# Cross-attention with routed experts: the first head group's maxima move into the projections, later groups' maximum rows travel by one copy and four transfers

## The reference, cut to what matters

```python
y_dca, y_main = y[:, -16:, :], y[:, :-16, :]      # y is the context: 16 and 496 rows
q = ln(x_norm @ Wq + bq, per head)                # 512 queries
k, v = ln(y_main @ Wk + bk), y_main @ Wv + bv     # 496 keys
k_dca, v_dca = ln(...), ...                       # 16 keys, of weights of their own
ctx = softmax(q k^T * 32**-0.5) v + softmax(q k_dca^T * 32**-0.5) v_dca
x = x + ctx @ Wo + bo
x = x + ffn(layernorm(x))                         # 7 routed experts, top 2, and one shared
```

## Time and profile before

| | |
|---|---|
| median of 3 runs | 995.12 us (993.21 to 996.1) |
| profiled execution | 995.3 us; its span in the trace 993.6 us |
| TensorE busy | 909.5 us, 92% of the span |
| VectorE, ScalarE, GpSimd busy | 636.0, 459.5, 563.9 us |
| mean granted clock of TensorE | 0.962 of full |

### The profile page before, as it was taken

The page is one execution under the profiler, slowest core; times in us unless marked ns, Lnnn a source line. Parts: engine busy times, 40 slices in busy tenths (PEclk is TensorE's granted clock), DMA queues, the critical chain, the costliest instruction groups (busy, mean ns, idle before and its releaser), DMA issues. The chain is left out here.

```text
span 993.6 us, 16827 instructions
## 1 busy us (share of the span) xinstructions
PE 909.5 (92%) x5047; PEld 406.6 (41%) x5048; DVE 636.0 (64%) x1019; ACT 459.5 (46%) x846; POOL 563.9 (57%) x487
## 2 busy tenths in 40 slices
PE   3889895799999999989999689999999999999898
PEld 1345442122221222246644245555555555555443
DVE  7888777588787988467776144554554444443388
ACT  3375665678877888722353022332233233323540
POOL 5465556367777775543127499989999920000372
PEclk9798998599999999999999799999999999999999
DMA  7234635445454532133425766666566643335676
GB/s 233 77 92 122 179 105 166 139 158 169 167 177 159 177 105 70 53 107 128 153 112 218 289 191 209 217 200 220 201 215 205 201 139 106 121 109 187 232 203 221
DMA packets 106059, 162.26 MB, mean 163 GB/s; under 512 B 12536, under 2 KB 55608, under 8 KB 105616
## 3 DMA queue, kind: packets, MB, share of 16 engines
q1 hardware_dynamic: 92768, 115.86, 35.9%
q0 software_dynamic: 12896, 45.10, 13.6%
q10 hardware_dynamic: 336, 0.57, 0.2%
HBM read 107.88 MB, written 53.48 MB: 162 GB/s over the span
## 5 line engine op out<-in xcount | busy, mean ns | idle before, releaser
L1089 ACT ACTIVATE p_t<-a_psT 128x512 f32<-128x512 f32 x256 | 138.9, 595 | 47.4 <-PE a_psT L1212 46.1
L1136 DVE TENSOR_REDUCE nm<-quad 128x4 bf16<-128x1984 f32 x60 | 133.9, 2231 | 35.7 <-PE quad L1197 35.7
L1905 ACT ACTIVATE e_xT<-quad 128x512 f16<-128x512 f32 x38 | 22.7, 597 | 229.9 <-PE quad L1969 229.9
L1979 PE MATMUL quad<-w_exp,e_xT 128*128 x456 | 107.2, 386 | 4.9 <-DVE e_xT L1933 2.6
L1039 POOL TENSOR_TENSOR p_sum<-p_t,p_t 128x512 f32<-128x512 f32 x64 | 81.1, 1275 | 53.2 <-ACT p_t L1089 53.0
L1979 PE MATMUL quad<-w_exp,e_uT 128*128 x456 | 104.6, 379 | 0.0
L1979 PE MATMUL e_psY<-w_exp,e_gT 128*128 x456 | 104.6, 379 | 0.0
L1212 PE MATMUL a_psT<-q_stk,k_stk 98*128 98x512 f16 x256 | 84.6, 401 | 11.2 <-ACT p_t L1089 9.4
L215 POOL TENSOR_TENSOR w_exp<-e_raw,w_exp 128x1024 f16<-128x1024 f32 x42 | 91.7, 2184 | 3.5
L1936 DVE SCALAR_TENSOR_TENSOR e_g<-quad,bias 128x512 f32<-128x512 f32 x38 | 26.3, 691 | 85.4 <-PE e_psGT L1969 80.5
L1936 DVE SCALAR_TENSOR_TENSOR e_u<-quad,bias 128x512 f32<-128x512 f32 x38 | 26.3, 691 | 73.9 <-PE quad L1979 73.9
(11 more groups left out here) (338 smaller groups left out, 1797.0 us busy)
## 6 DMA issues: line engine op xcount, KB each, us to landing
xs_dram<-zero SPq DMA_DIRECT2D x38, 256.0 KB, 6.9
bias<-in_L_ffn_bup_dram SPq DMA_DIRECT2D x38, 256.0 KB, 3.3
bias<-in_L_ffn_bgate_dram SPq DMA_DIRECT2D x38, 256.0 KB, 3.4
ys_dram<-e_y SPq DMA_DIRECT2D x38, 256.0 KB, 2.0
e_x<-xs_dram SPq DMA_DIRECT2D x36, 256.0 KB, 2.8
q_dram<-q_st SPq DMA_DIRECT2D x24, 256.0 KB, 3.0
k_dram<-k_st SPq DMA_DIRECT2D x24, 256.0 KB, 3.6
q_stk<-q_dram SPq DMA_DIRECT2D x64, 96.0 KB
```

Source lines behind the costliest of these rows:

```text
L1089: act.activation(probs(w, k), psT[:, k % 2], ACT.Exp, scale=SCALE / (QS * QS)).then_inc(s["exp"], 1)
L1136: dve.tensor_reduce(nm[:, i, :, 0:1].rearrange("p h o -> p (h o)"), psS[:, :, 0:NMAIN], AX.X, ALU.max, negate=True)
L1979: ins = pe.matmul(dst[:, :], stationary, moving, start=(k == 0), stop=(k == len(terms) - 1))
```

## The change

Group 0's scores are computed one head and one block at a time in `psD` by `first_score`, 16 in all, two for each of the last eight blocks of the projections; `first_max` reduces each. `first_max_rows` and four copies of ScalarE make group 0's rows inside `project`. The early scores now are those of group 1, blocks 0 and 1. `first_heads` is issued in batch 1 instead of the last one. In `attend`, ScalarE copies all of `psX` to a tile `m_row` once for each later group, and SP carries each head's two rows to `q_stk` by a transfer of its own, behind the loads of the group's fourth head. TensorE's order of turned pairs and sums is shifted by one place. Two loops that ran in hardware (VectorE, SP) are written out.

```diff
-MAX_EARLY = 4
+MAX_EARLY = 2
@@ project: first_heads
             for q in st_q + st_k:
-                sp.wait_ge(q, 3 * 16 * (B - 1))
+                sp.wait_ge(q, 3 * 16)
...
-                    if last and j == 1:
+                    if b == 1 and j == 2:
                         first_heads(sp)
@@ project: ScalarE, at the end
             back(B - 1, TB - 2)
+            act.wait_ge(g_["m_mm"], 1)
+            for h in range(HEAD_GROUP):
+                act.activation(g_["q_stk"][3 * HD:3 * HD + 2, h, :], psK[h * HD:h * HD + 2, :], ACT.Copy, scale=1.0 / QS).then_inc(g_["mrow"], 1)
             back(B - 1, TB - 1)
@@ project: VectorE, in mid behind the eviction of v, and in steps between front_a and front_c
+                if b >= B - 2:
+                    first_max(first_of(b, j) + 1)
...
+            def first_max(n):
+                i, h = divmod(n, HEAD_GROUP)
+                dve.wait_ge(g_["first_mm"], n + 1)
+                nm = g_["nm"][:, i, h, 0:2]
+                dve.tensor_reduce(nm[:, 0:1], psD[:, 0:NMAIN], AX.X, ALU.max, negate=True)
+                dve.tensor_reduce(nm[:, 1:2], psD[:, NMAIN:S], AX.X, ALU.max, negate=True).then_inc(g_["first_max"], 1)
...
+                    if b >= B - 2:
+                        first_max(first_of(b, j))
@@ project: TensorE, in mid behind the products of q, and in back between the turns of q and k
+                if b >= B - 2:
+                    first_score(first_of(b, j))
...
+                    if src is kn and between is not None:
+                        first_score(between)
...
+            def first_score(n):
+                i, h = divmod(n, HEAD_GROUP)
+                at_least(pe, g_["first_max"], n)
+                at = slice(h * HD, (h + 1) * HD)
+                pe.matmul(psD[:, :], g_["q_hi"][at, 0, i * P:(i + 1) * P], g_["k_hi"][at, 0, :], start=True, stop=True,
+                          tile_position=(h * HD, 0)).then_inc(g_["first_mm"], 1)
@@ attend: SP
+                if u % G == G - 1 and u >= G:
+                    sp.wait_ge(s["mrow"], copied(u // G))
+                    for h in range(G):
+                        sp.dma_start(q_stk[K3:KR, h, :], m_row[h * HD:h * HD + 2, :]).then_inc(row_put, 16)
@@ attend: ScalarE, once a group instead of four times max_row
+            def max_copy(gr):
+                act.wait_ge(s["m_mm"], gr + 1)
+                at_least(act, row_put, rows_of(gr - 1))
+                act.activation(m_row[:, :], psX[:, :], ACT.Copy, scale=1.0 / QS).then_inc(s["mrow"], 1)
@@ attend: TensorE
             def scores_t(w, k):
                 if k == 0:
                     pe.wait_ge(loaded[w % SLOTS], 32 * (w // SLOTS + 1))
-                    pe.wait_ge(s["mrow"], w + 1)
+                    at_least(pe, row_put, rows_of(w // G))
@@ attend: TensorE, the order of a period
                     scores(new, 1)
+                turned_pair(now, 0, 0)
                 if scored(old):
                     sums(old)
-                turned_pair(now, 0, 0)
+                turned_pair(now, 0, 1)
                 if scored(old):
                     third_sums(old)
                 if scored(new) and new:
                     scores(new, 2)
-                turned_pair(now, 0, 1)
+                turned_pair(now, 1, 0)
                 if scored(old):
                     last_sums(old)
-                turned_pair(now, 1, 0)
+                turned_pair(now, 1, 1)
                 if scored(old):
                     values(old, 2)
                 if scored(new) and new:
                     scores(new, 3)
-                turned_pair(now, 1, 1)
+                turned_pair(now, 2, 0)
                 if scored(old):
                     dca(old)
-                turned_pair(now, 2, 0)
+                turned_pair(now, 2, 1)
                 if scored(old):
                     values(old, 3)
-                turned_pair(now, 2, 1)
                 turned_pair(now, 3, 0)
```

More of the change, by code:

```diff
@@ L184, in build @@
         seen_max = sem("a_max")
+        first_mm = sem("a_first_mm")
+        first_max = sem("a_first_max")
+        m_mm = sem("a_m_mm")
+        mrow = sem("a_mrow")
         xs_zeroed = sem("xs_zeroed")
@@ L356, in w_view, with first_of @@
             return w.rearrange("p (h two d) -> p h two d" if natural else "p (two h d) -> p h two d", two=2, d=HD)
+        def first_of(b, j):
+            return 2 * (g_of(b, j) - (B - 2) * TB)
         def k_cols(w):
@@ L417, in _ @@
                              vf[b * NDCA:(b + 1) * NDCA, :].rearrange("p (h d) -> p h d", d=HD)).then_inc(s["dca_v_st"], 16)
-            with sp.Fori(1, B - 1) as b:
+            for b in range(1, B - 1):
                 steps(b, False)
@@ L817, in _ @@
             dca_norm()
-            with dve.Fori(1, B - 1) as b:
+            for b in range(1, B - 1):
                 steps(b, False, False)
             steps(B - 1, False, True)
-            dve.wait_ge(s["masks"], 6)
             for i in range(MAX_EARLY):
@@ L894, in dca_keys_turn, with back @@
                 ins.then_inc(s["dca_kT_t"], 1)
-            def back(b, j):
+            def back(b, j, between=None):
                 g = g_of(b, j)
                 for src, dst, rdy, used, dn in ((qn, psQT, "qn_r", "qa_r", "qT_t"), (kn, psKT, "kn_r", "ka_r", "kT_t")):
+                    if src is kn and between is not None:
+                        first_score(between)
                     pe.wait_ge(s[rdy], g + 1)
@@ L906, in back, with first_max_rows @@
                     ins.then_inc(s[dn], 1)
+            def first_score(n):
+                i, h = divmod(n, HEAD_GROUP)
+                if n == 0:
+                    pe.wait_ge(g_["hi_loaded"][0], 32)
+                    pe.wait_ge(s["dca_kT_r"], 1)
+                at_least(pe, g_["first_max"], n)
+                at = slice(h * HD, (h + 1) * HD)
+                pe.matmul(psD[:, :], g_["q_hi"][at, 0, i * P:(i + 1) * P], g_["k_hi"][at, 0, :], start=True, stop=True,
+                          tile_position=(h * HD, 0)).then_inc(g_["first_mm"], 1)
+            def first_max_rows():
+                pe.wait_ge(g_["first_max"], TB * HEAD_GROUP)
+                pe.wait_ge(s["k_ev"], NT)
+                for q in range(TB):
+                    ins = pe.matmul(psK[:, q * P:(q + 1) * P], g_["nm"][:, q, :, :].rearrange("p h o -> p (h o)"), ident_b[:, :], start=True, stop=True)
+                ins.then_inc(g_["m_mm"], 1)
             def early_scores(i):
                 if i == 0:
-                    pe.wait_ge(g_["hi_loaded"][0], 32)
+                    pe.wait_ge(g_["hi_loaded"][1], 32)
+                    pe.wait_ge(g_["first_max"], TB * HEAD_GROUP)
                     pe.wait_ge(s["q_ev"], NT)
@@ L916, in early_scores @@
                     at = slice(h * HD, (h + 1) * HD)
-                    ins = pe.matmul(psS[:, h], g_["q_hi"][at, 0, i * P:(i + 1) * P], g_["k_hi"][at, 0, :], start=True, stop=True, tile_position=(h * HD, 0))
+                    ins = pe.matmul(psS[:, h], g_["q_hi"][at, 1, i * P:(i + 1) * P], g_["k_hi"][at, 1, :], start=True, stop=True, tile_position=(h * HD, 0))
                 ins.then_inc(g_["s_mm"], 1)
@@ L932, in steps @@
                         dca_keys_turn()
+                    between = first_of(b, j) + 1 if b >= B - 2 else None
                     if last and j == TB - 1:
+                        back(b, j - 1, between)
                         early_scores(0)
-                    if j:
-                        back(b, j - 1)
+                        first_max_rows()
+                    elif j:
+                        back(b, j - 1, between)
                     elif not first:
-                        back(b - 1, TB - 1)
+                        back(b - 1, TB - 1, between)
             front(0, 0)
@@ L988, in scored, with rounds, copied, rows_of @@
             return 0 <= p < NG
+        def rounds(p):
+            return TB * (p - 1)
+        def copied(gr):
+            return G + gr
+        def rows_of(gr):
+            return 16 * G * gr
         def probs(n, k):
@@ L1106, in _ @@
                 n = early_of(p)
-                if scored(p - 1):
-                    for h in range(G):
-                        max_row(G * (p - 1) + h)
+                if scored(p - 1) and p - 1:
+                    max_copy(p - 1)
                 pair(p - 2, TB - 1, 1)
@@ L1132, in maxima @@
             def maxima(p, i):
-                dve.wait_ge(s["s_mm"], TB * p + i + 1)
-                at_least(dve, s["m_mm"], p)
+                if p == 1 and i < MAX_EARLY:
+                    return
+                dve.wait_ge(s["s_mm"], rounds(p) + i + 1)
+                dve.wait_ge(s["m_mm"], p)
                 dve.tensor_reduce(nm[:, i, :, 0:1].rearrange("p h o -> p (h o)"), psS[:, :, 0:NMAIN], AX.X, ALU.max, negate=True)
@@ L1190, in scores @@
             def scores(p, i):
+                if p == 1 and i < MAX_EARLY:
+                    return
                 if i == 0:
```

(7 more changed lines are left out.)

20 lines of the change are left out of this document (10 added, 10 removed).

## The result

The changed kernel takes 1085.8 us (median of 4 runs, 1084.13 to 1086.3) against 994.2 us before: ratio 1.091, 95% interval 1.0891 to 1.0929. The profiled execution took 1086.3 us with a span of 1084.6 us.

A forecast was written before the change was run, and what follows sets the result against it. TensorE was taken as the busiest engine, its waits deciding; a period grows from 15.09 to 19.1 us, fifteen cost 60 more. Sum: 995.3 - 6.6 + 60 = 1048.7, say 1049 us; range 1014 to 1086.

The forecast's parts named there:

- The rival with the deep queue: Attention: in ten periods with stores of zeros, transfers land 9.5 us after the group's last turned pair; 1088 us, chance 0.09.
- The landing: Between groups: the fourth transfer lands at T + 6.0 (4.9 to 9.5), T being the end of a group's last turned pair.
- The body of a turn: TensorE in attention: the rest of a period's work, from the next group's first turned pair to its last, takes 11.8 us.
- The clock: TensorE behind the new wait: drops to half clock in most periods, 1.3 us each (0 to 1.7).
- The row's full value: Profile of the kernel before: TensorE work at 1.2 GHz behind two waits, worth 1.7 us at full clock.
- VectorE's rival: Attention: transfers are cheap, VectorE sets a period of 15.1 us, 6 us won at the head; 989 us, chance 0.06.
- The forecast point of decision: Between groups: cheap transfers decide from a landing 3.7 us after the last turned pair, where fifteen periods cost 6.6 us.
- The end of `project`: End of the projections: the barrier moves from 174.88 to about 174.1, a gain of 0.8 us.
- The cover of the maxima: VectorE in `project`: waits hide most of the sixteen `first_max`, leaving 2.2 us; without any cover 12 us.
- I count nothing: Batch 1: earlier `first_heads` holds SP some 9 us, taken as no cost, 3 us if cover is thin.
- the first group: Start of attention: takes 11.5 us instead of 17.36, a gain of 5.8 us.
- the four row copies: ScalarE ahead of the last block's turned k and q: four copies delay GpSimd's last subtraction by 1.4 us.

The follow-up runs named there:

- (5): Changed kernel with two row transfers in place of four, same 8 KB, still behind the fourth head's loads: 1078.4 us.
- (8): Changed kernel with the row transfers issued by ScalarE on its own queue, SP issuing loads only: 1083.6 us.
- (4): Changed kernel with the four row transfers issued ahead of the fourth head's two loads instead of behind them: 1036.2 us.
- experiment 6: Changed kernel with two row transfers in place of four, issued ahead of the fourth head's loads: 1020.7 us.
- the warm kernel: Changed kernel with twelve products of overwritten result filling most of TensorE's wait for the transfers: 1060.6 us.
- (1): Changed kernel with four ScalarE row copies again and no transfers; new TensorE order and head part stay: 997.5 us, ratio 1.0017.
- head-only: Changed kernel with four ScalarE row copies and TensorE's old order, so only the head part is left: 996.1 us, ratio 1.0006.
- (10): Head part alone in three steps: alone 996.1 us; eight stack loads back in the last batch 988.6 us; then row copies last 989.6 us.
- the split one: Head part alone, with the eight stack loads of `first_heads` back in the last batch: 988.6 us, ratio 0.9932 of the kernel before.

## Why the prediction was right, and where it was off

Slower was forecast, for the reason that holds: four transfers that start at T, land about T + 6 and hold TensorE's queue, with the clock at half behind them. The size, 1049, was 37 us short of 1086, at the very edge of the range, and that it still lay inside is luck: three terms of a turn were each too small, and all in the same direction. The rival with the deep queue had 1088, nearer in number but not in kind: it wanted T + 9.5 in ten turns, and only the first turn came to that. By the prediction's own steps:

- *The landing.* Forecast T + 6.0; measured 6.0 to 6.3 in the last five turns, a mean of 6.8 over nine with zeros, 9.4 in the first, 6.8 over all fifteen. The reason given, that the first transfer queues behind head 3's loads and the fourth lands with it, held: half the issues changed the landing by 0.2 us or so (5), another queue not at all on the mean of the turns with zeros (6.8 in both, 8), a place ahead of the loads by 2.4 where no zeros are (4). The issue was 0.62 us each, not 0.48, which mattered little for that reason. As the prediction also had it, the queue is on the DMA engines and not SP's (8). The zeros were put among the rivals only; they cost 0.7 us in each of nine turns. Term: +0.8 us a turn.
- *The body of a turn.* Forecast 11.8 us from the pair to T. At full clock it is 12.4 (389.22 to 401.66 in the kernel of experiment 6). The 0.56 us wait for ScalarE did go, as said, but the step missed that another comes with the spread order: 0.75 us for `scaled_dca` ahead of `max_rows`, in 14 turns. +0.6.
- *The clock.* Forecast 1.3 us in most turns. What is left of the turn is 21.1 - 6.8 - 12.4 = 1.9; the warm kernel gives 1.7. The row's full value was the better one. Every wait here was 3.3 us or more and the clock fell behind each, though not always at once (the pair at 414.71 took 0.59 us, and the granted clock over the 3.5 us from there was 0.68). +0.6. These three make the 2.0 us a turn between 19.1 and 21.1, 30 us.
- *VectorE's rival.* The pair at T + 3.3 and a turn of 15.1 us if the transfers cost nothing; measured T + 2.7 and 15.22 (1), 15.13 to 15.26 (6). The forecast point of decision, a landing at T + 3.7, was reached in turns without zeros (3.67 in 4, 2.7 in 6) and in some with them (3.3 in 6).
- *The end of `project`.* Forecast 174.1, measured 180.7. The cover of the maxima held: a block takes 7.9 us where it took 7.85. The step that failed is "I count nothing" for the earlier `first_heads`, with 3 us if cover is thin: it cost 5.3 us of waiting for x and 1.4 (head-only) to 2.8 us (changed) of low clock behind that wait. With the stack loads away (10) the rest of the step came out: attention starts at 173.6 (forecast 174.1), the first group takes 11.9 us (forecast 11.5), and it ends at 185.5, where 192.24 - 6.6 = 185.6 was the forecast. Only the four row copies, taken at 1.4, cost 0.34. The first exponential, expected 3 to 5 us earlier, is 2.4 us later in the changed kernel (182.09, before 179.72) and 4.7 us earlier in the split one (175.02).

30 us from the turns and 7.4 from the head are the 37.6 us between 1048.7 and the profiled 1086.3.

What the change wins is at the head, some 6 to 7 us, and it was hidden by the load order there; later groups' transfers gain nothing over four copies by any form tried. Even where the transfers vanish a turn in the new order is about 15.1 us: TensorE's 14.0 us of work and two waits for VectorE, 0.35 us for the maxima and 0.75 us for `scaled_dca`. VectorE itself stands for 2.1 us of such a turn (386.40 to 401.66 in experiment 6), each time for TensorE's scores, so it is the chain between the two that sets the pace. The new order gives nothing here, and the 1.9 us that ScalarE saves have no taker. The old order with one copy and hidden transfers was not tried.

Open: how the zeros hold the transfers, and why longer in some turns than in others (experiment 6 mostly alternates between 3.4 and 5.0 us); and why TensorE's low clock behind the wait for x cost 2.8 us in the profile of the changed kernel and 1.4 in that of the head-only one, whose projections are the same.

## What to carry to other kernels

A small transfer can cost what lies in the DMA engines at the time it starts: look which bulk loads and stores were issued in the few us ahead of it, on any queue, and put the small one first. When loads are moved earlier, find the next load in the same issuing queue and ask when its data is needed; a queue that seems to run a block ahead may be held for 9 us. And a wait on the busiest engine is often paid twice, once in full and once in the clock behind it, which may show one block later and on another engine.

## What was not expected of the hardware

- A two-row transfer of 2 KB from SBUF to SBUF takes 0.62 us to issue on SP, where a 2 KB load took 0.43. Four of them ahead of the loads, in turns without zeros, have landed 1.1 us after the last issue ended.
- Another issuing engine doesn't help a transfer past loads. In turns without zeros the last one is there 3.4 to 4.4 us after the end of its issue on ScalarE's queue and 2.2 to 2.4 us on SP's behind the loads in the changed kernel, at about the same distance from T.
- The length of one wait doesn't tell whether the granted clock falls behind it. It was at 1.2 GHz behind a wait of 1.95 us in the kernel of experiment 4 and at full speed for 7 us behind one of 2.71 us in that of experiment 6:

```profile
219.30 1.01 PE L1284 MATMUL a_psT<-q_stk,k_stk 98*128 98x512 f16 x2 [1.95 <-issue]
```

```profile
218.38 0.59 PE L1284 MATMUL a_psT<-q_stk,k_stk 98*128 98x512 f16 x2 [2.71 <-issue]
```
